# Two-layer graph kernel: ScalarE issues the x1 stores and the loads of the residual rows in the first layer

## The reference

```python
norm2  = jnp.linalg.norm(x, axis=1, keepdims=True)
cos    = beta[0] * (x @ x.T) / (norm2 @ norm2.T + 1e-07)
P      = jax.nn.softmax(cos + (1.0 - adj) * -1000000000.0, axis=1)
x      = _layernorm(x + P @ x)                  # first layer
x      = _layernorm(x + adj @ (x @ weight))     # second layer
```

## Time and profile before

| | us |
|---|---|
| median of 3 runs | 504.02 (503.45 to 504.99) |
| the profiled execution | 508.47 |
| its span, first to last instruction | 506.7 |
| PE busy | 467.8 (92%) |
| DVE busy | 382.3 (75%) |
| ACT busy | 315.2 (62%) |
| POOL busy | 62.2 (12%) |

### The profile page before, as it was taken

One profiled execution on the slowest core, in us unless ns is written; L12 is line 12 of the kernel. 1 busy time (PEld: TensorE's weight loads), 2 busy tenths in 40 slices (PEclk: granted clock), 3 DMA queues, 4 the chain that ended last, 5 costly groups with the idle time before them and its releaser, 6 DMA issues.

```text
span 506.7 us, 8872 instructions
## 1 busy us (share of the span) xinstructions
PE 467.8 (92%) x3491; PEld 303.3 (60%) x3491; DVE 382.3 (75%) x630; ACT 315.2 (62%) x358; POOL 62.2 (12%) x71
## 2 busy tenths in 40 slices
PE   0749999999799999999989999999989999999994
PEld 0526676666467577677666666666664445544484
DVE  4797989999799999999999999999993022111253
ACT  4568888899589789978978987898882000000000
POOL 4310000111020110202102010210110000000011
PEclk9979999999999999999999999999999999999998
DMA  8999999999979969996995999690033100111111
GB/s 207 102 105 122 117 113 124 133 105 134 149 93 126 164 105 85 143 146 81 168 124 86 91 165 156 54 191 3 1 89 141 43 21 22 41 43 41 43 40 44
DMA packets 101690, 50.20 MB, mean 99 GB/s; under 512 B 69376, under 2 KB 98208, under 8 KB 101664
## 3 DMA queue, kind: packets, MB, share of 16 engines
q0 software_dynamic: 17952, 16.78, 39.7%
q1 hardware_dynamic: 83424, 33.05, 32.1%
q10 hardware_dynamic: 288, 0.07, 0.1%
HBM read 77.40 MB, written 22.82 MB: 198 GB/s over the span
## 4 chain that ended last, share of the span: by engine, by line
PE 60%; DMA 24%; DVE 7%; issue 3%; ACT 3%; SPq 1%; POOL 1%; POOLq 0%; ACTq 0%; DVEq 0%
PE psum L934 21%; DMA adj_bytes<-in_adj 15%; PE psum L876 13%; PE psum L880 7%; DMA adjT<-adj_bytes 6%; PE psum L855 6%; PE psum L854 6%; PE psum L853 6%; DVE el L646 3%; DVE E L638 2%; DMA xres<-in_x 2%; PE psum L944 1%; DMA adjT<-in_x 1%; ACT E L423 1%; ACT eh L432 1%
## 5 line engine op out<-in xcount | busy, mean ns | idle before, releaser
L876 PE MATMUL psum<-xaug,eh 128*128 128x257 f16 x1024 | 186.1, 276 | 17.2 <-DVE uT L535 7.1
L423 ACT ACTIVATE E<-psum,sc 128x1024 f32<-128x1024 f32 x128 | 154.1, 1204 | 53.2 <-PE psum L855 50.5
L880 PE MATMUL psum<-xaug,el 128*128 128x129 f16 x1024 | 176.9, 222 | 0.0
L638 DVE SCALAR_TENSOR_TENSOR E<-E,adjT 128x1024 f32<-128x1024 f32 x128 | 159.1, 1243 | 19.1 <-ACT E L423 16.5
L646 DVE SCALAR_TENSOR_TENSOR el<-E,eh 128x1024 f16<-128x1024 f32 x128 | 159.1, 1243 | 0.0
L432 ACT ACTIVATE eh<-E 128x1024 f16<-128x1024 f32 x128 | 134.0, 1047 | 6.6 <-DVE E L638 6.5
L876 PEld LDWEIGHTS psum<-xaug,eh 128*128 128x128 f16 x1024 | 99.7, 98 | 48.0 <-DVE h L684 8.5
L934 PE MATMUL psum<-adjT,uT 128*128 128x512 fp8e4 (+1 forms) x576 | 112.1, 356 | 0.0
L880 PEld LDWEIGHTS psum<-xaug,el 128*128 128x128 f16 x1024 | 100.8, 98 | 12.9 <-issue 0.2
L853 PE MATMUL psum<-uT 128*128 (+1 forms) x256 | 98.0, 383 | 0.0
L854 PE MATMUL psum<-uT 128*128 (+1 forms) x256 | 97.9, 383 | 0.0
(11 more groups left out here) (71 smaller groups left out, 162.9 us busy)
## 6 DMA issues: line engine op xcount, KB each, us to landing
adj_bytes<-in_adj POOLq DMA_DIRECT2D x31, 512.0 KB, 11.9
adjT<-in_x SPq DMA_DIRECT2D x4, 512.0 KB, 7.0
xres<-in_x SPq DMA_DIRECT2D x8, 256.0 KB, 7.7
q_row<-norms SPq DMA_DIRECT2D x8, 256.0 KB, 8.9
x_rows<-x SPq DMA_DIRECT2D x8, 256.0 KB, 3.5
E<-x_rows SPq DMA_DIRECT2D x8, 256.0 KB, 3.0
out<-E SPq DMA_DIRECT2D x16, 128.0 KB, 2.2
x_parts<-x1p SPq DMA_DIRECT2D x7, 256.0 KB, 6.9
```

What stands on the lines that cost most here:

```text
L423: nc.scalar.activation(E[:, m % RING, :, :], S[m % 2], ACT.Exp, bias=col(C_BB), scale=col(C_BS)).then_inc(e_done, 1)
L638: nc.vector.scalar_tensor_tensor(out=e, in0=e, scalar=EPRE, in1=mask_bytes(b, m), op0=ALU.mult, op1=ALU.min).then_inc(masked, 1)
L876: return nc.tensor.matmul(O[t][:, 0:XC], eh[:, s, a, cols], xaug[:, j, :], start=start, stop=stop)
L880: return nc.tensor.matmul(O[t][:, 0:D + 1], el[:, s, a, cols], xaug[:, j, 0:D + 1], start=False, stop=False)
```

## The change

In the first layer ACT issues three transfers of each block that SP issued. The store of x1 follows the upper part at m = 15. The load of `xres` follows the split of m = 7, with a wait until the former residual rows were used (the semaphore `chain`). The store of `x1p` is issued one block later than the part is made: in block b, after the split that ACT does at m = 1, for rows of block b-2, and only after POOL's subtraction for these rows. For the last two blocks SP issues the stores as before. The residual rows of block 0 stay with SP.

```diff
@@ sync
                 if b + 1 < NB:
                     load_mask(b + 1)
-                store_x1(b - 1)
-                load_xres(b)
-                if b < NB - 1:
-                    store_x1p(b - 1)
@@ scalar
+            def store_x1(b):
+                act.wait_ge(x1_done, b + 1)
+                act.dma_start(x1_v[b], x1[:, :, :]).then_inc(x1_stored, 16)
+
+            def store_x1p(b):
+                act.wait_ge(x1_split, b + 1)
+                act.dma_start(x1p_v[b], x1p[:, :, :, :].rearrange("p t a d -> p t (a d)")).then_inc(x1p_stored, 16)
+
+            def load_xres(b):
+
+                act.wait_ge(chain, 6 * b - 3)
+                act.dma_start(rows_in_twos(xres[:, :, :]), x_v[b]).then_inc(xres_in, 16)
+
             for b in range(1, NB):
                 for m in range(NP):
                     if m == LAG:
                         read_out(b - 1)
                     exp_pair(b, m)
                     split_hi(b, m - 1)
+                    if m == 1 and b > 1:
+                        store_x1p(b - 2)
+                    if m == 7:
+                        load_xres(b)
                     if m in (11, 12, 13, 14):
                         normalise(b - 1, [m - 11])
                     if m == 15:
                         split_x1_hi(b - 1)
+                        store_x1(b - 1)
```

More of the change, by code:

```diff
@@ L284, in store_x1p @@
                 sp.dma_start(x1p_v[b], x1p[:, :, :, :].rearrange("p t a d -> p t (a d)")).then_inc(x1p_stored, 16)
-            def load_xres(b):
-                sp.dma_start(rows_in_twos(xres[:, :, :]), x_v[b]).then_inc(xres_in, 16)
             load_q_row(0)
```

## The result

| | before | changed |
|---|---|---|
| median us | 504.12 (503.45 to 504.99, 4 runs) | 517.74 (515.62 to 521.65, 4 runs) |
| ratio | | 1.0265 (95%: 1.0226 to 1.0304) |
| profiled execution, us | 508.47 | 521.65 |
| its span, us | 506.7 | 519.8 |
| read-out of block 2, of block 7, us | 121.78, 341.78 | 127.03, 355.14 |

The changed kernel is slower by 13.6 us. The forecast was +10.5 us, 514.5, with a range of 509.0 to 522.0: right in sign, in place and in its main mechanism, 3 us short in size. Two executions on record that took far longer, 1749.44 us of the kernel before and 1007.92 us of e7, are left out of every median and ratio here.

A forecast was written before the change was run, and what follows sets the result against it. PE was taken as the bound. The delay of 10.0 us at block 7's read-out plus 0.5 for PE's clock gave +10.5 us, on the median of 504.02 us 514.5 us; range 509.0 to 522.0.

The forecast's parts named there:

- place: ACT at m = 1 in blocks 2 to 6, none in block 7; read-out of block 7 +10.0 us.
- main mechanism: ACT's wait for POOL's subtraction delays PE's read-out: block 2 8.2 us late, blocks 3 to 6 44.8 us a period.

The follow-up runs named there:

- e7: The changed kernel with the store of the parts one pair later, at m = 2 in place of m = 1: 507.80 us, ratio 1.0080.
- a2: The changed kernel, unchanged, traced a second time: 519.14 us, span 517.3 us.
- e4: The changed kernel with POOL's subtraction put between the second and third of its four casts: 501.08 us, ratio 0.9942.

## What to carry to other kernels

Before a wait is put on an engine of the main loop, read when the thing waited for is really done, and from what point its chain starts: here ACT came to the store 2.5 to 5.2 us before POOL was through (up to 7.3 us in a2), and as that chain starts from the very read-out which it delays, the loss came again in each block. What it costs is set by how late that thing is and by the work between the wait and the next point on which the bound depends, so the same DMA five pairs later is free. And where a trace shows POOL with an independent computation behind waits for DMA, as here, put the computation into the gap: this alone took 0.9% off the kernel before.

## What the hardware showed beside that

A DMA issued by ACT without an open wait took nothing from its computing here (the exponential beside it has its usual 1.21 us, and in e4, with all three transfers on ACT, the periods are the undisturbed 42.57 us), and goes out ahead of computing that stands before it in the program: the x1 store (L474) was issued at 111.97, during the exponential that had begun at 111.83, while the split and the upper part that stand before it started at 112.93 and 113.88. An open wait is another matter: it held back all that stands behind it, by 5.73 us in block 2, and by 7.86 us in a2.

Behind a stop of PE of 4.04 us its clock fell, when PE was already working again, and the loss lay in the work behind the stop; in a2 the clock from 122.2 to 126.2 us averages 0.88, so there it fell before the stop of 6.18 us was over. The length of one stop doesn't tell whether the clock falls. The stop in block 3 of the changed kernel was 2.08 us long, and the clock fell behind it; that of block 4 was 2.26 us long, and it did not, and neither did it around the 2.91 us before 136.05 in the kernel before (the earlier trace rows shows the stretch from 134). In the changed kernel, the stops of blocks 3 and 4 and the stretches around them:

```profile
174.55 0.39 PE L864 MATMUL psum<-uT 128*128 x1 [2.08 <-ACT E L416]
...
221.15 0.39 PE L864 MATMUL psum<-uT 128*128 x1 [2.26 <-ACT E L416]
```
```profile
176.00:178.00 2.00, 1.54 (x7) 0.59 (x6) 2.00 (x5) 2.00 (x3) 0.00 (x0) 0.50 1.08 179
...
222.00:224.00 2.00, 0.74 (x5) 0.21 (x4) 2.00 (x4) 2.00 (x5) 0.00 (x0) 1.00 1.07 117
```

And the stop in the kernel before:

```profile
136.05 0.28 PE L876 MATMUL psum<-xaug,eh 128*128 128x257 f16 x1 [2.91 <-DVE el L646]
```
